# Value products two key tiles behind the weights, key and value scaling on VectorE, and the first output bias on TensorE

## What is computed

```python
x = x + gated_deltanet(layernorm(x))    # first layer
x = x + moe(layernorm(x))               # 16 experts, top 4, and a shared one
x = x + attention_b(layernorm(x))       # causal, rmsnorm and rope on q and k
x = x + moe(layernorm(x))

# gated_deltanet
q, k, v = x @ Wq + bq, x @ Wk + bk, x @ Wv + bv
k = k / (norm(k) + 1e-6);  beta = sigmoid(x @ Wbeta + bbeta)
for t in range(512):                    # per sequence and head, S is 16 x 16
    delta = v_t - S @ k_t
    S = S + beta_t * outer(delta, k_t)
    o_t = S @ q_t
return o @ Wo + bo

# attention_b
attn = softmax(mask(q @ k.T * hd ** -0.5));  return (attn @ v) @ Wo
```

## Time and profile before

| what | us |
|---|---|
| median of 3 runs | 5514.33 |
| lowest and highest | 5511.0, 5519.31 |
| the profiled execution | 5518.57 |
| its span in the trace | 5517.3 |
| DVE busy | 4095.3 |
| PE busy | 3331.9 |
| POOL busy | 1776.0 |

### The profile page before, as it was taken

How to read it: one execution, slowest core, us unless ns; L and a number is a source line. 1 busy time by engine, 2 the same in 40 slices (tenths; PEclk the granted TensorE clock), 3 DMA queues, 4 the chain that set the end, 5 groups by cost and what they waited for, 6 DMA issues and landing times.

```text
span 5517.3 us, 71359 instructions
## 1 busy us (share of the span) xinstructions
PE 3331.9 (60%) x20252; PEld 2339.9 (42%) x20252; DVE 4095.3 (74%) x10422; ACT 1938.4 (35%) x4713; POOL 1776.0 (32%) x2760
## 2 busy tenths in 40 slices
PE   6312055374544743245267887886698878887875
PEld 2201033253322532135254655564466545664664
DVE  1899988999889998999645666767566667665533
ACT  3111022142221321023034655564456555554332
POOL 1110012502444124410535143314611353226534
PEclk8655576697666976579678998998899999998997
DMA  1310001263213532146352333421133334333787
GB/s 50 120 42 8 0 17 36 93 178 114 69 54 104 168 106 73 58 149 176 109 177 79 104 111 108 122 89 63 64 102 101 104 111 131 116 100 122 228 274 235
DMA packets 425088, 588.15 MB, mean 107 GB/s; under 512 B 57344, under 2 KB 301184, under 8 KB 424576
## 3 DMA queue, kind: packets, MB, share of 16 engines
q1 hardware_dynamic: 375552, 449.31, 27.0%
q0 software_dynamic: 49152, 134.28, 7.3%
HBM read 374.97 MB, written 208.40 MB: 106 GB/s over the span
## 4 chain that ended last, share of the span: by engine, by line
DVE 44%; PE 29%; issue 10%; POOL 9%; ACT 4%; DMA 3%; SPq 1%; DVEq 0%; ACTq 0%; POOLq 0%
PE psum L1061 5%; DVE rec L1125 5%; DVE rec L1127 5%; DVE skb L1130 5%; DVE rec L1138 4%; DVE rec L1141 4%; POOL xbuck L1708 4%; DVE region L1133 3%; DVE psum L1243 3%; PE psum L917 3%; PE psum L1069 2%; PE psum L969 2%; DVE acc L1410 2%; POOL yg L1718 2%; PE psum L861 2%
## 5 line engine op out<-in xcount | busy, mean ns | idle before, releaser
L1061 PE MATMUL psum<-xgT,w 128*128 128x128 f32 x5296 | 768.0, 291 | 83.6 <-issue 28.9
L1718 POOL DMA_INDIRECT yg<-ybuck,words x512 | 534.6, 1044 | 871.9 <-DMA ybuck<-yrow 517.5
L1061 PEld LDWEIGHTS psum<-xgT,w 128*128 128x128 f32 x5296 | 699.8, 205 | 136.0 <-issue 94.7
L1069 PE MATMUL psum<-w_w2T,hid 128*128 x1324 | 452.7, 426 | 307.7 <-DVE hid L1394 229.5
L1243 DVE CUSTOM_DVE_ANT_0 psum<-psum,xo 128x128 f32<-128x128 f32 (+3 forms) x1024 | 473.6, 518 | 146.5 <-PE psum L938 145.2
L1708 POOL DMA_INDIRECT xbuck<-srow,words x512 | 524.4, 1024 | 152.8 <-issue 124.4
L849 PE MATMUL psum<-w_ident,xn 128*128 128x128 f32 x512 | 108.4, 349 | 759.4 <-ACT xn L1427 749.6
L1555 ACT ACTIVATE region<-psum 128x512 f32<-128x512 f32 (+3 forms) x1024 | 402.7, 438 | 327.8 <-PE psum L957 318.5
L1689 POOL TENSOR_SCALAR_AFFINE_SELECT region<-region 128x128 f32<-128x128 f32 x1024 | 290.5, 299 | 611.0 <-ACT region L1555 597.2
L1590 ACT ACTIVATE xgT<-psum 128x256 f32<-128x256 f32 x662 | 252.8, 382 | 653.8 <-PE psum L1051 652.7
L1079 DVE SCALAR_TENSOR_TENSOR sil<-sil,psum 128x128 f32<-128x128 f32 (+1 forms) x465 | 137.3, 295 | 449.1 <-ACT sil L1599 412.3
(11 more groups left out here) (201 smaller groups left out, 7447.5 us busy)
## 6 DMA issues: line engine op xcount, KB each, us to landing
w<-in_w13T SPq DMA_DIRECT2D x662, 256.0 KB, 3.2
xg<-xbuck SPq DMA_DIRECT2D x662, 128.0 KB, 2.9
ybuck<-yrow SPq DMA_DIRECT2D x662, 128.0 KB
xbuck<-x SPq DMA_DIRECT2D x40, 512.0 KB, 5.3
x_scratch<-res SPq DMA_DIRECT2D x64, 256.0 KB, 2.1
acc<-x_scratch SPq DMA_DIRECT2D x128, 128.0 KB
xbuck<-srow,words POOLq DMA_INDIRECT x512
yg<-ybuck,words POOLq DMA_INDIRECT x512
```

Source lines behind the costliest of these rows:

```text
L1061: o = e.matmul(psum[:, mi, half], w13[I % 3][:, k, half], xgT[I % 2][:, k, :], start=(k == 0), stop=(k == 1), skip_group_check=True)
L1069: o = e.matmul(psum[:, mi, 0:D], hid[hi][:, 0:128], w2T[:, bass.ds(expert.pop(I), 1), :].rearrange("p a b -> p (a b)"), start=True, stop=True)
L1718: e.indirect_dma_start(yg[y % 5], None, ybuck[g % 2][0:TILES_OF[g] * 128, :], bass.IndirectOffsetOnAxis(ap=posu[g % 2][:, J - ROWS0[g], k: ...
```

## The change

1. `p_norm` on POOL is gone. DVE multiplies the reciprocal itself and then, in the new stage `p_scale`, keys and values in eight pieces of 128x512, with room for other stages between the pieces. `l_turn` waits for the eight pieces.
2. `o_in` has no POOL part. `o_add` waits for the DMA of `xo` itself, and `o_proj` gets a third matmul that adds the bias: a row of ones (one partition) times boA.
3. `w_pv` of a key tile is put after the dots of the second tile behind it, across the borders of head groups, and `w_out` one turn after the last of a group. `close` is gone. There are sixteen buffers P, cut to the size of their tile; two of them lie over `qkr`, and `b_qk_out` gets a wait for that, which asks for no more than the `w_out` ahead of it on ACT has waited for already.

```diff
@@ project
             put("p_norm", k)
             yield LIGHT
+            for i in range(8):
+                yield LIGHT
+                put("p_scale", k, i)
+            yield LIGHT
@@ weigh
                         pend = (k, kt, a, mi)
-                        if a == 3 and kt:
-                            put("w_pv", k, kt - 1)
                         yield
+                    ready.append((k, kt))
+                    if len(ready) > 2:
+                        yield from values()
                 put("w_exp", *pend)
                 misc.give(pend[-1], "we", 16 * k + 16)
                 weighed.add(hg)
-                closing.append(Strand(close(hg)))
-
-        def close(hg):
-            k = 4 * b + hg
-            yield
-            yield
-            put("w_pv", k, NQ - 1)
-            yield
-            put("w_out", k)
+            while ready:
+                yield
+                yield from values()
+        ready = []
+
+        def values():
+            k, kt = ready.pop(0)
+            put("w_pv", k, kt)
+            if kt == NQ - 1:
+                yield
+                put("w_out", k)
...
-    P = [part(10240 + i * 512, [512]) for i in range(8)]
+    P = [part((10240, 12288, 13824, 14848)[kt] + a * n, [n]) for kt, n in enumerate((512, 384, 256, 128)) for a in range(4)]
@@ l_turn, PE
-                pe.wait_ge(s["bpool"], 4 * (2 * q + g) + 4)
+                pe.wait_ge(s["bnorm"], 8 * (2 * q + g) + 8)
@@ o_proj, PE
-                    o = e.matmul(psum[:, mi, 256:512], otc[ci][:, k, :], woA[:, k, :], start=(k == 0), stop=(k == 1))
-                o.then_inc(s["ow"], 1)
+                    e.matmul(psum[:, mi, 256:512], otc[ci][:, k, :], woA[:, k, :], start=(k == 0), stop=False)
+                e.matmul(psum[:, mi, 256:512], ones[:, :], boA[0:1, :], start=False, stop=True).then_inc(s["ow"], 1)
@@ p_norm and p_scale, DVE
                 e.reciprocal(f, f).then_inc(s["brec"], 1)
+                dv.wait_ge(s["brec"], 2 * k + 1)
+                e.tensor_tensor(f, f, flat2[k % 2][:, 0, :], ALU.mult).then_inc(s["brec"], 1)
+            elif name == "p_scale":
+                k, i = u
+                four, f = slice(i // 2 * 4, i // 2 * 4 + 4), flat2[k % 2][:, 1 - i % 2, :]
+                st = stage[k % 2][:, 2 * (i % 2), four, :]
+                dv.wait_ge(s["brec"], 2 * k + 2)
+                e.tensor_tensor(st, st, bc(f, 1, 4), ALU.mult).then_inc(s["bnorm"], 1)
@@ o_add, DVE
-                dv.wait_ge(s["rb"], r)
+                dv.wait_ge(s[f"xo{oi}"], v)
@@ b_qk_out, ACT
                 ac.wait_ge(s["lo"], max(i - 3, 0))
+                ac.wait_ge(s["pv"], 64 * (i // 4))
@@ w_exp, ACT
-                ac.wait_ge(s["pv"], max(w - 7, 0))
+                ac.wait_ge(s["pv"], max(w - 15, 0))
@@ p_norm and o_in, POOL
-                e.tensor_tensor(f[:, 1, :], f[:, 1, :], f[:, 0, :], ALU.mult).then_inc(s["bpool"], 1)
-                po.wait_ge(s["bpool"], 4 * k + 2)
-                e.tensor_tensor(st[:, 0, :, :], st[:, 0, :, :], bc(f[:, 1, :], 1, 16), ALU.mult).then_inc(s["bpool"], 1)
-                e.tensor_tensor(st[:, 2, :, :], st[:, 2, :, :], bc(f[:, 0, :], 1, 16), ALU.mult).then_inc(s["bpool"], 1)
...
-                po.wait_ge(s[f"xo{oi}"], v)
-                e.tensor_tensor(xo[oi], xo[oi], boA[:, :], ALU.add).then_inc(s["rb"], 1)
```

More of the change, by code:

```diff
@@ L312, in attention @@
             yield 1
-        turning, closing, out, weighed = [], [], set(), set()
+        turning, out, weighed = [], set(), set()
         def largest():
@@ L373, in weigh @@
                 weighed.add(hg)
-                closing.append(Strand(close(hg)))
-        def close(hg):
-            k = 4 * b + hg
-            yield
-            yield
-            put("w_pv", k, NQ - 1)
-            yield
-            put("w_out", k)
+            while ready:
[8 more added lines that the diff above has]
+                put("w_out", k)
         heads_of, weights = Strand(largest()), Strand(weigh())
-        while not (heads_of.done and weights.done and all(t.done for t in closing)):
-            for t in closing + [weights] + turning + [heads_of]:
+        while not (heads_of.done and weights.done):
+            for t in [weights] + turning + [heads_of]:
                 t.step()
@@ L969, in tensor @@
                     o = e.matmul(psum[32 * a:32 * a + 32, 6, kt * 128:SEQ], vb[:, kt, k % 4 * 4 + a, :],
-                                 P[w % 8][:, 0:n], start=(kt == 0), stop=(kt == NQ - 1), skip_group_check=True)
+                                 P[w % 16][:, 0:n], start=(kt == 0), stop=(kt == NQ - 1), skip_group_check=True)
                     o.then_inc(s["pv"], 1)
```

23 lines of the change are left out of this document (8 added, 15 removed).

## The result

| | before | changed |
|---|---|---|
| median of 4 runs, us | 5516.82 | 5451.55 |
| lowest and highest | 5511.0, 5524.23 | 5447.6, 5461.31 |
| span of the profiled execution | 5517.3 | 5446.2 |

The ratio is 0.9884, with a 95% interval from 0.9864 to 0.9903: 65 us less (54 to 75). The forecast was 5443, and its range went from 5395 to 5485.

A forecast was written before the change was run, and what follows sets the result against it. DVE was taken to bound the scan, latencies the stretch between, PE's stops the attention. 8.1 + 17.6 + 16.6 + 4 + 25 = 71.3 us off 5518.57 gave 5447, forecast as 5443 us for the runs' median; range 5395 to 5485.

The forecast's parts named there:

- the lock in the scan: Scan: POOL's multiplications lock out DVE's operations with two SBUF inputs for a whole instruction; scaling there cost DVE 47.6 us.
- the cover in the attention: Attention: value products placed later give PE 2.4 to 2.8 us of cover, once, until POOL's mask has caught up.
- scaling, k = 2 to 7: Scan: DVE regains 47.6 us lost to POOL and pays 30.0 us for the pieces, a gain of 17.6 us.
- scaling, k = 0 and 1: Start, where nothing covers the scalings: 3.4 us gained for k = 0 and 4.7 for k = 1, together 8.1.
- bias in the scan: Scan: 10 us from the lock, 5.6 from waits for `xo`, 3 from gathers, less 2 for PE's matmul: 16.6 us.
- last rows: Behind the scan: POOL's additions leave a latency chain and PE matmuls enter; 4 us gain, bounds -6 and 10.
- value products: Attention: 34 us of PE's mask stops go, less 5 for `w_out` and 4 for other waits: 25 us.
- first scan step near 150 us: Sign in the changed kernel's trace: the first scan step comes near 150 us instead of 157.9.
- four long first stops: Attention: four stretches start with one stop of 8 to 10 us; 2.5 us cover and small stops go, 16 in all.
- Rival 1: Attention: POOL's queue paces the stretches and PE merely waits later, so no gain there: 5468 us; chance 0.20.
- Rival 3: Attention: ACT is late copying bank 6 at 48 head-group borders, 2.1 us each, 101 in all: 5569 us; chance 0.04.
- Rival 2: Attention: stops at a sequence's end shrink too, 85 of 107.9 us go: 5383 us; chance 0.09.

The follow-up runs named there:

- the early bias matmul: Changed kernel with the bias matmul moved ahead of its row tile's transposes (wrong sums, only time read): 5460.63 us, ratio 0.9897.
- one tile: Changed kernel with the value products one key tile behind the weights, not two: 5487.85 us, ratio 0.9932.
- the mask on PE: Kernel before with scaling and bias parts, old value order, causal mask added by a third PE product: 5388.43 us; its last rows took 238.0 us.
- the kernel that scales twice: Kernel before with two more POOL products of 128x2048 after each scaling (only time read): 5581.28 us, ratio 1.0115.

## Why the prediction was right, and where it wasn't

By the runs 65 us were gained (54 to 75), and I had forecast 71.3. Both mechanisms that carry the sum, the lock in the scan and the cover in the attention, are shown by the experiments. That the total came so near is in part luck: four terms were too large by 18 us together, and one was too small by 6.5. By stages, with the means of like kernels:

| term | forecast | measured |
|---|---|---|
| scaling, k = 2 to 7 | 17.6 | 16.4 |
| scaling, k = 0 and 1 | 8.1 | 2.3 (end of the prologue; the part of k = 0, 3.4, can't be read) |
| bias in the scan | 16.6 | 10.8 |
| last rows | 4 | -1.6 (six profiles of 214.6 to 223.1, mean 219.8, against six of 215.7 to 221.2, mean 218.2; left out: the one of 238.0 us at the low clock, and the early bias matmul) |
| value products | 25 | 31.5 |
| sum | 71.3 | 59.4 |

**The profile flattered the sum.** The span of the changed kernel's profile is 71.1 us shorter, nearly my number. 5.9 of it are the short head, where TensorE was granted 0.89 against 0.86 before. The forecast's sign "first scan step near 150 us" came true (150.7) by that alone in good part: the end of the prologue gave 1.3 us between these two profiles. The subtraction stayed below 1 us, as the forecast asked, and the scan was 35 us shorter in this pair, 27 by the means.

**Scaling.** The mechanism and the size hold: DVE's two-input operations gave back 49.2 us, where I had 47.6 (a slip: 8.5 + 0.3 is 8.8 and not 8.6, and the sum 48.0), pieces stand 0.60 us apart, and twice the POOL work costs 49.5 us more.

**Prologue.** The step that failed is "the pieces end near 144.7 and the transpositions start just then, where they started at 149.33". Before, 16 of these 64 transpositions had been made during POOL's multiplications; only 48 started at 149.33. DVE's copies free the banks that PE transposes into, and they now stand behind the eight pieces in DVE's queue. The list in front of the prediction shows just that: after the reciprocal came the copies, and now the pieces come first. The timelines of PE, before, then after:

```profile
140.29 3.65 PE L870 MATMUL psum<-w_ident,region 128*128 128x128 f32 x16 [0.56 <-DVE region L1113]
...
149.33 7.72 PE L870 MATMUL psum<-w_ident,region 128*128 128x128 f32 x48 [5.39 <-POOL region L1652]
```

```profile
139.69 10.17 PE L879 MATMUL psum<-w_ident,region 128*128 128x128 f32 x64 [5.88 <-DVE region L1130]
```

2.45 us of the 4.7 went there. The 3.4 us for k = 0 can't be seen in heads that vary by 14 us.

**Bias in the scan.** The lock's 10 us were right (10.7), and the 3 for the gathers too (3.9). The step that failed is "only POOL's 0.83 us goes: 7 x 0.8 = 5.6". With POOL's addition gone and the bias matmul out of the way DVE still waits 13.0 us there, against 14.0 in the mean of the kernels with POOL's bias: the row tile itself comes that late, and POOL's addition had lain beside that wait. So 1 us went and not 5.6. The matmul behind the products adds some 3 us (16.6 in the mean), near the 2 that I had charged.

**Last rows.** The 4 us of gain, a difference between two estimates, didn't come. PE is busy for 139.2 us there, 17 more than the 122.4 of before, for the sixteen matmuls of one row; whether that is the reason was not tested.

**Value products.** 31.5 us against 25, the one term that was too small. Stops fell by 33, as I had it by place (34), but this agreement is of little worth: other stops of PE rose by as much, and the gain came out of PE's busy time (28 to 31 us), where waits lie hidden. I had charged 5 us for `w_out`; PE's waits for that copy are 10.5 us, and were 7.2. They and the mask's 74.6 us lie just outside the forecast's signs (below 10, and 50 to 70). Of the four long first stops, the one of 8.9 us stayed (9.7), those of 10.2 and 8.2 became 3.6 and 4.5, and the last, 8.18 us in the stretch from 5075 to 5106 us, became two of 2.8 and 3.5. Rival 1, that POOL takes all stops back, is what one tile does; with two it doesn't. Rival 3, the border of head groups, didn't come. Rival 2, that most of the stops are to be had, has its measure in the mask on PE.

## What to carry to other kernels

The waits that a view names can be less than what a cause costs. Where instructions overlap, a wait can lie under the duration of the one before it and count as busy time, and a long stop can be followed by a lower clock; a kernel without the cause (here without the mask) tells the whole. Before a stall is covered by moving its user, ask what it would cost to do the work that it waits for on the engine that waits: here 1024 small matmuls cost 31 us and took away a stall worth 143, where the cover cost 12 and brought 44. And when work moves from one engine's queue to another's, look at what now stands behind it there, and not only at when it ends.

## What the runs showed of the hardware

- In the kernel that scales twice, each of POOL's 24 multiplications of 128x2048 in the scan held up one two-input operation of DVE until it ended, and the twelve that had come in cost 4.1 us each; reductions beside them took their usual 0.67 us.
- A 128x128 bf16 product put behind two others into the same bank showed 222 ns as its duration and cost 30 ns of time in the old order and 28 in the new. The duration of a small matmul is no price.
- The head of the program took 126.6 to 140.9 us in nine executions of the same instructions, with a granted clock of 0.89 in the shortest and 0.82 in the longest. A single profile of each kernel can't carry a difference of 6 us there.
